# A two-layer model on one core: the shared expert moved ahead of the routed ones, with the gathers and weighted sums in a stage of their own

## The reference, cut to what matters

```python
def _mlp(x, w_fc, w_proj):
    return jnp.square(jax.nn.relu(x @ w_fc.T)) @ w_proj.T
...
out = jnp.zeros_like(flat)
for e in range(E):                       # E = 8; combine is zero but for the 2 chosen experts
    out = out + _mlp(flat, w_fc[e], w_proj[e]) * combine[:, e:e + 1]
out = out + _mlp(flat, shared_fc, shared_proj)
...
g = _silu(_L0_ffn_ref(xn, ...))
x = x + s * g                            # s is the attention of layer 0
```

## Time and profile before

| what | value |
|---|---|
| median of 3 runs | 2270.74 us (2268.06 to 2274.66) |
| span of the profiled execution | 2261.7 us |
| median less span: what lies around it | 9.0 us |
| PE busy | 2007.7 us (89%) |
| DVE busy | 1718.4 us (76%) |
| ACT busy | 1121.3 us (50%) |
| POOL busy | 1615.8 us (71%) |
| mean granted clock of PE | 0.954 of full speed |

### The profile page before, as it was taken

One profiled execution on the slowest core, in us unless ns is written; L12 is line 12 of the kernel. 1 busy time (PEld: TensorE's weight loads), 2 busy tenths in 40 slices (PEclk: granted clock), 3 DMA queues, 4 the chain that ended last, 5 costly groups with the idle time before them and its releaser, 6 DMA issues. The chain is left out here.

```text
span 2261.7 us, 33617 instructions
## 1 busy us (share of the span) xinstructions
PE 2007.7 (89%) x8183; PEld 1155.2 (51%) x8183; DVE 1718.4 (76%) x2770; ACT 1121.3 (50%) x2031; POOL 1615.8 (71%) x1394
## 2 busy tenths in 40 slices
PE   5799999999999999999999999999996997454676
PEld 4355555555555555555555555555554665242354
DVE  7777777777777777777777777777776997258996
ACT  1355554555555545555555455555555886142533
POOL 4277777777777777777777777777776996714785
PEclk9899999999999999999999999999998999675889
DMA  5101000111010001110100011101003442101000
GB/s 192 34 22 26 22 21 21 26 27 25 21 26 22 21 21 26 27 26 21 26 22 21 21 25 27 26 21 26 22 21 111 138 142 76 50 14 49 0 14 23
DMA packets 70435, 84.75 MB, mean 37 GB/s; under 512 B 9272, under 2 KB 47480, under 8 KB 69760
## 3 DMA queue, kind: packets, MB, share of 16 engines
q1 hardware_dynamic: 50176, 57.08, 10.4%
q0 software_dynamic: 7552, 20.98, 2.8%
q10 hardware_dynamic: 12672, 6.29, 0.9%
HBM read 30.84 MB, written 18.87 MB: 22 GB/s over the span
## 5 line engine op out<-in xcount | busy, mean ns | idle before, releaser
L1085 POOL TENSOR_TENSOR psum_k<-psum_k,probs 128x512 f32<-128x512 f32 x768 | 959.6, 1279 | 80.5 <-ACT probs L1047 77.1
L1047 ACT ACTIVATE probs<-ps_s 128x512 f32<-128x512 f32 x1024 | 593.4, 597 | 732.8 <-PE ps_s L986 686.7
L1102 DVE TENSOR_REDUCE mxh<-ps_m 128x1 f32<-128x512 f32 x1044 | 683.7, 681 | 275.8 <-PE ps_m L940 262.4
L949 PE MATMUL ps_v<-probs,V 128*64 128x512 f32 x2048 | 488.8, 603 | 0.0
L985 PE MATMUL ps_s<-Q,K 128*128 128x512 f32 x1024 | 460.5, 450 | 0.0
L940 PE MATMUL ps_m<-K,Q 128*128 128x512 f32 x1044 | 420.4, 404 | 31.0 <-DVE mxh L1102 30.3
L986 PE MATMUL ps_s<-Q,K 72*128 72x512 f32 x1024 | 406.5, 397 | 0.0
L1085 POOL TENSOR_TENSOR psum_k<-probs 128x512 f32<-128x512 f32 x128 | 160.8, 1276 | 301.9 <-ACT probs L1047 301.9
L985 PEld LDWEIGHTS ps_s<-Q,K 128*128 128x128 f32 x1024 | 192.7, 188 | 300.8 <-issue 197.2
L949 PEld LDWEIGHTS ps_v<-probs,V 128*64 128x64 f32 x2048 | 127.0, 136 | 246.5 <-issue 156.9
L940 PEld LDWEIGHTS ps_m<-K,Q 128*128 128x128 f32 x1044 | 199.7, 191 | 100.4 <-DVE mxh L1102 53.3
(11 more groups left out here) (251 smaller groups left out, 2669.2 us busy)
## 6 DMA issues: line engine op xcount, KB each, us to landing
K<-K SPq DMA_DIRECT2D x132, 128.0 KB
Q<-Q SPq DMA_DIRECT2D x132, 128.0 KB, 2.4
rows<-zeros SPq DMA_DIRECT2D x4, 1536.0 KB, 15.1
r_x_raw<-rows SPq DMA_DIRECT2D x24, 256.0 KB, 3.4
results<-r_y_row ACTq DMA_DIRECT2D x24, 256.0 KB, 2.3
x_tok<-in_X SPq DMA_DIRECT2D x4, 512.0 KB, 5.5
x<-in_X SPq DMA_DIRECT2D x4, 512.0 KB, 5.2
out_x<-out_t SPq DMA_DIRECT2D x8, 256.0 KB, 2.3
```

The costliest lines, as they stand in the source:

```text
L949: nc.tensor.matmul(ps_v[hf][rows, :], V[par][:, kt, rows], probs[:, k % NPR, :], start=kt == 0, stop=kt == KT - 1).then_inc(pv_done, 1)
L1047: nc.scalar.activation(probs[:, k % NPR, :], ps_s[x][:, :], ACT.Exp, scale=SCALE).then_inc(p_done, 1)
L1085: nc.gpsimd.tensor_tensor(acc, probs[:, (k - 2) % NPR, :] if kt == 1 else acc, probs[:, k % NPR, :], ALU.add).then_inc(add_done, 1)
L1102: nc.vector.tensor_reduce(mxh[:, i % 8, i // 8:i // 8 + 1], ps_m[i % 2][:, :], AX.X, ALU.max).then_inc(m_done, 1)
```

## The change

`expert_tiles` for the shared expert now runs before that of the routed ones, and ends with the shared result in `g.gate`: after PE's transposes into `ps_2`, DVE copies each sequence from PSUM to `g.gate` (four copies of 128x1024), and PE's next transposes wait for that copy (`rows_done`). The gathers, the weighted sums and the silu leave `expert_tiles` and become a new stage, `combine`, behind the routed experts. There the first sum adds choice 0 to `g.gate` instead of to PSUM. The wait between choice 0 and choice 1 (`sum_step`) now stands behind the wait for the gathers of choice 1.

```diff
@@ program
             with ExitStack() as stage:
+                expert_tiles(nc, stage, g, False)
+            with ExitStack() as stage:
                 expert_tiles(nc, stage, g, True)
             with ExitStack() as stage:
-                expert_tiles(nc, stage, g, False)
+                combine(nc, stage, g)
@@ expert_tiles, PE
                 if b:
-                    pe.wait_ge(sum_step, b)
+                    pe.wait_ge(rows_done, b)
@@ expert_tiles, ACT: the four silu are gone; POOL: the 64 gathers are gone
...
@@ expert_tiles, DVE
+            for b in range(B):
+                v.wait_ge(y_ready, NO + b + 1)
+                nc.vector.tensor_copy(g.gate[:, b * T:(b + 1) * T], ps_2[:, :]).then_inc(rows_done, 1)
+
+
+def combine(nc, ctx, g):
...
+    with nc.Block() as block:
+        @block.gpsimd
+        def _(pool):
+            for b in range(B):
+                for k in range(2):
+                    for t in range(b * TPB, (b + 1) * TPB):
+                        nc.gpsimd.indirect_dma_start(y[k][:, t, :], None, g.results[:, :],
+                                                     bass.IndirectOffsetOnAxis(ap=g.pos[:, k, t:t + 1], axis=0)).then_inc(y_in[b][k], 16)
+
+        @block.vector
+        def _(v):
             gate = g.gate[:, :].rearrange("p (t d) -> p t d", d=D)
             for b in range(B):
-                v.wait_ge(y_ready, NO + b + 1)
                 for k in range(2):
                     v.wait_ge(y_in[b][k], TPB * 16)
+                    if k:
+                        v.wait_ge(sum_step, b + 1)
                     for t in range(b * TPB, (b + 1) * TPB):
-                        other = ps_2[:, t % TPB * P:(t % TPB + 1) * P] if k == 0 else gate[:, t, :]
-                        ins = nc.vector.scalar_tensor_tensor(gate[:, t, :], y[k][:, t, :], g.weight[:, k, t:t + 1], other, ALU.mult, ALU.add)
+                        ins = nc.vector.scalar_tensor_tensor(gate[:, t, :], y[k][:, t, :], g.weight[:, k, t:t + 1], gate[:, t, :], ALU.mult, ALU.add)
                     ins.then_inc((sum_step, sum_done)[k], 1)
-                    if k == 0:
-                        v.wait_ge(sum_step, b + 1)
+
+        @block.scalar
+        def _(act):
+            for b in range(B):
+                act.wait_ge(sum_done, b + 1)
+                rows = g.gate[:, b * T:(b + 1) * T]
+                nc.scalar.activation(rows, rows, ACT.Silu).then_inc(gate_done, 1)
```

More of the change, by code:

```diff
@@ L383, in expert_tiles @@
         oT_all = sb("s_oT", [P, NT], F32)
-        y = [sb(f"y{k}", [P, TILES, D], F32) for k in range(2)]
     ps_z = [pb(f"{tag}ps_z{i}", [P, CH]) for i in range(NZ)]
@@ L412, in expert_tiles @@
     else:
[L413 to L416, removed]
+        rows_done = sem("shared_rows_done")
     def is_int(i, value):
@@ L616, in _ @@
                     act.wait_ge(y_out[s], 16 * NI)
[L617 to L621, removed]
         @block.gpsimd
@@ L625, in _ @@
             if not routed:
[L627 to L631, removed]
                 return
@@ L726, in _ @@
                 return
+            for b in range(B):
+                v.wait_ge(y_ready, NO + b + 1)
+                nc.vector.tensor_copy(g.gate[:, b * T:(b + 1) * T], ps_2[:, :]).then_inc(rows_done, 1)
+def combine(nc, ctx, g):
+    sb, pb, sem = g.scope(ctx)
+    y = [sb(f"y{k}", [P, TILES, D], F32) for k in range(2)]
+    y_in = [[sem(f"y_in{b}{k}") for k in range(2)] for b in range(B)]
+    sum_step = sem("sum_step")
+    sum_done = sem("sum_done")
+    gate_done = sem("gate_done")
+    with nc.Block() as block:
[8 more added lines that the diff above has]
+        def _(v):
             gate = g.gate[:, :].rearrange("p (t d) -> p t d", d=D)
             for b in range(B):
-                v.wait_ge(y_ready, NO + b + 1)
                 for k in range(2):
                     v.wait_ge(y_in[b][k], TPB * 16)
+                    if k:
+                        v.wait_ge(sum_step, b + 1)
                     for t in range(b * TPB, (b + 1) * TPB):
-                        other = ps_2[:, t % TPB * P:(t % TPB + 1) * P] if k == 0 else gate[:, t, :]
-                        ins = nc.vector.scalar_tensor_tensor(gate[:, t, :], y[k][:, t, :], g.weight[:, k, t:t + 1], other, ALU.mult, ALU.add)
+                        ins = nc.vector.scalar_tensor_tensor(gate[:, t, :], y[k][:, t, :], g.weight[:, k, t:t + 1], gate[:, t, :], ALU.mult, ALU.add)
                     ins.then_inc((sum_step, sum_done)[k], 1)
-                    if k == 0:
-                        v.wait_ge(sum_step, b + 1)
+        @block.scalar
[4 more added lines that the diff above has]
+                nc.scalar.activation(rows, rows, ACT.Silu).then_inc(gate_done, 1)
 def layer0_attention(nc, ctx, g):
```

## The result

| | before | after |
|---|---|---|
| first set of runs, median of 5 | 2274.32 us (2268.06 to 2274.83) | 2281.76 us (2281.03 to 2282.31) |
| span of the profiled execution | 2261.7 us | 2279.6 us |
| a second set (experiment 6), median | 2218.89 us (13 runs) | 2280.27 us (4 runs) |

In the first set, the one the prediction is held against, the change makes the kernel slower by 7.4 us or 0.4%: the ratio is 1.0041, 95% interval 1.0027 to 1.0055. The prediction was 2287.8 us, and slower. The later sets change what that ratio means, and they are told with the experiments. First the two traces of the first set. This is the view by stretches of the kernel after: start:end, length, busy time and count on PE, PE's weight loads, DVE, ACT and POOL, then granted clock, DMA share and GB/s. The stretches are the shared stage, the routed stage, `combine` and layer 1.

What follows compares the result with a forecast made beforehand. It took no engine to bound the shared stage, where the gathers delayed PE's signals. Shared stage 63.6 plus `combine` 88.8 minus the old 135.3 gave +17.1 us: span 2278.8, median 2287.8 us, range 2274 to 2306.

Steps and rivals of the forecast that it cites:

- blocks without the stall: Shared stage: relus 1.40 us apart, the last starting at 47.4 us instead of 111.0; gain 63.6 us.
- Shared stage 63.6: New shared stage: 52.0 us to the first transposes plus an 11.6 us tail, against 135.26 us before.
- the copies: Shared stage's tail: four DVE copies of 128x1024 from PSUM, each taken as 1.23 us from an addition of that size.
- Routed stage 198.6: Routed experts' stage: forecast unchanged at 198.60 us.
- `combine` 88.8: New stage behind the routed experts: 85.3 us of bare gathers, last sums, silu and handing over, plus 3.5 us of contention.
- the term for contention in `combine`: `combine`: DVE's sums delay gathers, 0.5 us for each of seven bursts, 3.5 us; bounds nothing and 15.3 us.
- the 85.3 of that bound: `combine` without contention: last rows there at 81.7 us, then eight sums, the silu, handing over and meeting.
- with 9.0 us around it to the median: Whole kernel: the distance from the profiled 2261.7 us to the median of 2270.7, added again to the forecast span.
- the first rival: Shared stage: the stall belongs to the shared expert and stays, so 63.6 us are not gained; 2351 us, chance 0.06.
- the burst of 64 gathers holds back PE's signals: Shared stage before: forecast's reading of PE's late signals; moving the gathers away takes back a stall of 63.6 us.
- Faster gathers: Rival, `combine`: the 0.30 us between gathers vanishes without busy neighbours, 19 us go; 2269 us, chance 0.08.
- a faster layer 1: Rival, layer 1: PE, rested before it, runs at full clock; up to 28 us go, 2260 us, chance 0.03.

Runs made afterwards that it cites:

- experiment 6: The kernel after, unchanged, run beside the kernel before on another chip: 2280.27 us (4 runs), ratio to the kernel before 1.0278.
- experiment 1: The kernel after with 64 more gathers, read from rows into unread tiles, beside the shared blocks in the stage that now runs first: 2305.56 us.
- experiment 2: The kernel before, with POOL starting its gathers only when ACT has written the last chunk's shared result: 2271.0 us (4 runs), ratio 1.0224.
- experiment 5: The kernel before, unchanged, run again with a profile on a second chip: 2220.15 us (8 runs), shared stage 89.98 us.
- experiment 7: The kernel after with 64 more gathers of rows beside the shared blocks, repeated on a second chip: 2305.61 us, kernel before beside it 2218.89.
- experiment 10: The kernel before, unchanged, with a profile, on the second chip: 2217.48 us.
- experiment 11: The kernel before, unchanged, with a profile, on a third chip: 2219.87 us.
- experiment 12: The kernel after with 64 more gathers of rows beside the shared blocks, a third time, on a third chip: 2303.89 us, kernel before 2220.84.
- experiment 4: The kernel before, with POOL waiting for each gather to land before issuing the next: 2324.63 us.

## Why the prediction was right, and where it was not

**Right: the sum over the first set's trace, with some luck.** Forecast from profile to profile +17.1 us, measured 2279.6 - 2261.7 = +17.9. The terms: blocks without the stall, last relu at 47.4 us, measured 47.3. Shared stage 63.6, measured 62.7; the copies took 1.224 us each (taken: 1.23), and three of the four sets of transposes ran at the full clock instead of two. Routed stage 198.6, measured 199.0. `combine` 88.8, measured 86.2. That the total is off by only 0.8 us is luck in part: the two stages of the sum came out 3.4 us shorter than forecast, and 4.2 us that the sum did not have came in from the stages around them, where no cause is known. The median after fell 6.0 us below the forecast, well inside the range. The range's ends, 2274 and 2306, are not quite what its terms add up to: about 2275 and 2311 if each is taken whole.

**Wrong: the term for contention in `combine`.** 3.5 us were set for DVE's sums delaying gathers. The gathers took 940 to 999 ns beside 64 sums: nothing. Where the blocks' operations run beside gathers, some are delayed: in experiment 1 the longest is 1437 ns, near the 1.45 us of the earlier trace rows, and 64 gathers cost 63.7 us for 60.5. The same code and sums, with the gathers behind the blocks (experiment 2) and beside them (experiment 5), as least, median, most:

```profile
L631 POOL DMA_INDIRECT y<-results,pos x64: 941/945/996, 1963.7 to 2042.5; - x64
```

```profile
L630 POOL DMA_INDIRECT y<-results,pos x64: 943/948/1453, 1908.3 to 1991.1; - x64
```

So the delay is the blocks' and not the sums'; which of the blocks' operations does it was not separated. The lower bound, nothing, was the right value. That `combine` still took 0.9 us more than the 85.3 of that bound is mostly POOL at its end, told in the last section.

**Wrong: how the profile stands to the median.** The step "with 9.0 us around it to the median" took the whole of 2270.7 - 2261.7 for what lies around a span. The kernel after shows what does: 2281.76 us for a span of 2279.6, 2.2 us. The profiled execution of the kernel before must itself have been quicker than all timed ones: 2261.7 + 2.2 = 2263.9 us, against 2268.06 for the fastest. That is 6.8 us below the 2270.7 the prediction started from, and it is the term that was mis-sized: 2.2 and not 9.0 us. It accounts for the median after being 2281.8 and not 2287.8. With the two further runs the median before rose to 2274.3, another 3.6 us, so that +17.9 between the profiles became +7.4 between the medians. In which stage the timed executions before lost their extra time, no trace shows.

**Half right: the stall.** It left with the change, as forecast, and the first rival (2351 us) did not come. But "the burst of 64 gathers holds back PE's signals" was said of the kernel and holds, if at all, of the first place. On three chips the same burst runs beside the same blocks and holds back nothing (experiments 1, 5, 7, 10, 11, 12). There the argument's gain, 63.6 us for the stall, does not exist: the stage is bounded by the gathers at 90.0 us, and the change costs 62.7 + 86.2 - 90.0 = 58.9 us in those stages, 61.4 us in all. Even in the first place, by the stage of experiment 5, the most that mending the stall in the old order could give back was 135.3 - 90.0 = 45.3 us, since the gathers would then end last. What the change lays bare is larger than that under either condition; the sign does not hang on the stall, its size does.

**The rivals.** The rule of the Trainium skill ("SBUF — State Buffer", section "SBUF: two separate sides") that a transfer and PE cannot slow one another agrees with the three healthy chips: 33.00 us of PE busy in 33.00 us with 25 or 26 gathers beside. The conclusion drawn from it, that the stall would move along with the shared expert, was refuted by one trace, the kernel after in the first set; the runs of that code on the healthy chips, which have no stall anyway, add nothing. The rule itself is not refuted by it, since the change moved the stage away from the routed experts as well as from the gathers. Faster gathers did not come (0.30 us between two, 19.2 us in all, as before), nor a faster layer 1 (clock 0.80 both times).

**What stays open.** What makes the stall. It was seen in the first set alone, and whether the chip or the time set that apart is not known. The gathers are its likeliest partner: it fills their stretch, the kernel after is free of it, and the lost reports follow the gathers in both kernels. But the change also moved the stage, and the experiment that was to separate the two never ran where the stall is. Waiting for each gather, other transfers in their place, more completions and half the gathers were tried only on healthy chips. No version was found that beats both kernels: of all that ran, the kernel before on a healthy chip is the fastest, and in the first place it is still the faster of the two.

## What to carry to other kernels

A stall that one trace shows may belong to the chip or the hour as much as to the kernel: before spending a change on it, run the unchanged kernel elsewhere and later. Missing reports in the trace are a reason to do so at once. And before giving up an overlap to be rid of a stall, price the stage as it would be with the overlap and without the stall: here 90.0 us against 149.0, so the overlap was worth more than the stall in both conditions. Take the distance of a profile from the median as two numbers, what surrounds the span and how this execution stands among its like.

## What had not been expected of the hardware

The same program takes 2217 to 2223 us on three chips and 2268 to 2275 in another set, with nearly all of the difference between the profiles in one stage, while a program without gathers beside the shared blocks takes the same 2277 to 2282 in both sets that it ran in.

And POOL does not leave a stage with its last gather. The end of `combine` in the kernel after, then POOL's wait there (engine and line, total, times, longest):

```profile
2053.64 0.94 POOL L732 DMA_INDIRECT y<-results,pos  x1 [0.30 <-issue]
2056.09 2.19 DVE L744 SCALAR_TENSOR_TENSOR x_tok<-y,weight,x_tok 128x128 f32<-128x128 f32 x8 [7.77 <-DMA y<-results,pos]
2058.31 1.06 ACT L752 ACTIVATE x_tok<-x_tok 128x1024 f32<-128x1024 f32 x1 [18.89 <-DVE x_tok L744]
2060.44 0.38 SPq L1395 DMA_DIRECT2D x<-in_X  x1
```

```profile
POOL mhalf L1451 <- issue: 5.9, 1, 5.9
```

POOL's last gather ended at 2053.64 + 0.94 = 2054.58 and its first instruction of layer 1 ran 5.9 us later. In between the trace has one instruction of POOL called DRAIN, which ended at 2059.88, 5.3 us behind the last gather. The silu had ended at 2059.37. In the earlier trace rows, where POOL was long done, the next stage began 0.26 us behind the silu; here it began 1.07 us behind it. So the end of this stage was POOL's own, by about 0.8 us. Experiments 1 and 4 show the same more plainly, since POOL there waits for the last landing first: DRAIN then took 5.28 us and the stage ended with it, at 91.0 us where 83 had been forecast, and at 194.0. In the kernel before on a healthy chip the two ends nearly meet, POOL 5.5 us behind its last gather and the silu 0.5 us before the next stage. For a stage that ends with gathers, then, 5.3 us behind the last one belong in the sum, and what the other engines do in them costs nothing.
